# Edge phases of a graph network on one core: no loops, tiles gathered once into a ring, one-hots moved to ScalarE

## The reference

```python
# layer 1, 8 heads
score = einsum('ehd,ehd->eh', q[dst], k[src]) / sqrt(32)
alpha = exp(score - segment_max(score, dst)[dst]) / segment_sum(...)[dst]
out   = segment_sum(alpha[..., None] * v[src], dst)
# layer 3, 4 heads
e   = leaky_relu(e_src[src] + e_dst[dst], 0.2)
a   = exp(e - segment_max(e, dst)[dst]) / segment_sum(...)[dst] * dist
out = segment_sum(ft[src] * a, dst)
```

## Time and profile before

| | |
|---|---|
| median of 3 runs | 9977.47 us |
| the profiled execution | 9991.05 us |
| its span | 9989.3 us |
| busy PE, DVE, POOL, ACT | 73%, 59%, 44%, 34% |
| first edge phase (`att`) | 534 to 3943 us |
| second edge phase (`gat_att`) | 5487 to 8689 us |
| last experts (`sexp`) | 8950 to 9846 us |

### The profile page before, as it was taken

The page is one execution under the profiler, slowest core; times in us unless marked ns, Lnnn a source line. Parts: engine busy times, 40 slices in busy tenths (PEclk is TensorE's granted clock), DMA queues, the critical chain, the costliest instruction groups (busy, mean ns, idle before and its releaser), DMA issues. The chain is left out here.

```text
span 9989.3 us, 143724 instructions
## 1 busy us (share of the span) xinstructions
PE 7296.0 (73%) x33600; PEld 5271.7 (53%) x33600; DVE 5876.5 (59%) x16050; ACT 3420.6 (34%) x10075; POOL 4441.4 (44%) x4446
## 2 busy tenths in 40 slices
PE   3877887887888788535955677777777777659993
PEld 2555555555555555334743444545445545458873
DVE  3467777777777777752124555555555555663332
ACT  1256555555565564222422111111111111222220
POOL 2045555555555553052034655655555556440004
PEclk6989889888898888757977666766676766759996
DMA  4455555555555554444345333333333333335555
GB/s 142 159 151 154 148 153 151 146 151 148 152 153 149 149 151 132 140 144 132 119 143 170 86 81 81 82 81 82 83 82 82 82 82 82 78 118 178 178 178 160
DMA packets 814099, 1276.19 MB, mean 128 GB/s; under 512 B 274566, under 2 KB 585110, under 8 KB 812734
## 3 DMA queue, kind: packets, MB, share of 16 engines
q0 software_dynamic: 272448, 833.22, 30.5%
q1 hardware_dynamic: 540755, 432.95, 14.5%
HBM read 1070.02 MB, written 211.92 MB: 128 GB/s over the span
## 5 line engine op out<-in xcount | busy, mean ns | idle before, releaser
L694 POOL DMA_INDIRECT att_kv<-kv,att_idx x1872 | 1850.1, 988 | 1912.3 <-issue 1475.6
L694 POOL DMA_INDIRECT gat_att_vst<-ft,gat_att_idx x1872 | 1877.6, 1003 | 1340.6 <-DVE gat_att_score L956 723.7
L772 PE MATMUL gat_att_pag<-gat_att_msg,gat_att_S 128*128 128x260 f32 x3744 | 1466.6, 531 | 31.1 <-DVE gat_att_msg L978 9.1
L730 PE MATMUL att_pqd<-sum_acc,att_ST 128*128 x3744 | 1136.1, 431 | 390.9 <-ACT att_ST L816 295.5
L772 PE MATMUL att_pag<-att_msg,att_S 128*128 128x264 f32 x3744 | 1160.5, 436 | 84.4 <-DVE att_msg L978 42.4
L730 PEld LDWEIGHTS att_pqd<-sum_acc,att_ST 128*128 128x128 f32 x3744 | 769.6, 214 | 602.2 <-issue 480.5
L772 PEld LDWEIGHTS gat_att_pag<-gat_att_msg,gat_att_S 128*128 128x128 f32 x3744 | 888.2, 263 | 347.2 <-issue 153.4
L816 ACT CAST gat_att_ST<-gat_att_pST 128x256 bf16<-128x256 f32 x936 | 348.1, 372 | 2110.3 <-remote 1032.9
L772 PEld LDWEIGHTS att_pag<-att_msg,att_S 128*128 128x128 f32 x3744 | 692.6, 206 | 372.6 <-issue 166.9
L727 PE MATMUL gat_att_pqd<-sum_ed,gat_att_ST 128*128 x5616 | 372.1, 171 | 634.0 <-ACT gat_att_ST L816 436.9
L727 PEld LDWEIGHTS gat_att_pqd<-sum_ed,gat_att_ST 128*128 128x128 bf16 x5616 | 335.5, 106 | 941.3 <-issue 860.8
(11 more groups left out here) (474 smaller groups left out, 11913.9 us busy)
## 6 DMA issues: line engine op xcount, KB each, us to landing
sexp_w<-in_L_ffn_w_dram SPq DMA_DIRECT2D x112, 1024.0 KB
att_kv<-kv,att_idx POOLq DMA_INDIRECT x1872
gat_att_vst<-ft,gat_att_idx POOLq DMA_INDIRECT x1872
top_row<-tok SPq DMA_DIRECT2D x106, 256.0 KB
ytok<-top_y SPq DMA_DIRECT2D x106, 256.0 KB
kv<-qkv_row SPq DMA_DIRECT2D x50, 520.0 KB
sexp_row<-stok SPq DMA_DIRECT2D x56, 260.0 KB
sy<-sexp_y SPq DMA_DIRECT2D x56, 256.0 KB
```

Of the source, the lines that this page charges most:

```text
L694: pool.indirect_dma_start(row, None, rows_t, IndirectOffsetOnAxis(ap=idx[:, k, 2 * p + i:2 * p + i + 1], axis=0)).then_inc(s_g[p % R], 16)
L730: t = pe.matmul(pqd[p % 2][:, i * D:i * D + D], lhs, acc[:, bass.ds(b + 1, 1), 0:D], start=True, stop=True)
L772: t = pe.matmul(pag[p % 2][:, 0:AW], S[:, gs % RG, 2 * p + i, :], msg[:, p % 2, i, :], start=(i == 0), stop=(i == 1))
```

## The change

- `prepare_edges` also makes a list of source nodes by tile (`srcN`, one column for each of the 1680 tiles), for each slot pair the place of its tile pair in a ring of 24 and its number, and for each tile pair the number of the last slot pair that uses it (`free`).
- `edge_phase` has no loop any more: all 119 steps of groups are written out on every engine, so that all semaphore values and most addresses are constants.
- In `gat`, POOL gathers each tile pair once (1680 gathers in place of 1872) into a ring of 24 pairs of tiles. It waits for the message of the last slot pair that used the place (`s_msg` against a register from `free`), and tells of arrivals in order, three pairs behind, by a semaphore `s_here`. DVE reads from registers which place holds its slot pair, for the front (`ring`) and for the message (`back`), two slot pairs to a TENSOR_LOAD.
- In `gat`, ACT makes the one-hots as in `att`.
- In `att`, there are two product buffers, and the product waits for the reduction before the last one.
- In `switch_experts` the token rows are issued ahead of the weights.

```diff
+                sp.dma_start(nsrc[0:TN, :, :], dr["src"].rearrange("a (b t e) -> (a t) b e", t=TN, e=P)).then_inc(s_nat, 16)
...
+                    if b < NT // TN:
+                        sp.dma_start(dr["srcN"][:, b * TN:b * TN + TN], tnat[:, s, 0:TN]).then_inc(s_st[s], 16)
+                    if b == 2:
+                        sp.wait_ge(s_ring, 1)
+                        sp.dma_start(dr["ring"].rearrange("(a c) n -> a c n", a=1), ring[:, :, :]).then_inc(s_copy, 16)
+                        sp.dma_start(dr["free"], free[:, :]).then_inc(s_copy, 16)
...
+                    t = pe.transpose(pt[s][:, 2, 0:TBS], natd[0:TBS, s, :], c.ident[0:TBS, 0:TBS])
+                    if b < NT // TN:
+                        t = pe.transpose(pt[s][:, 3, 0:TN], nf[0:TN, s, :], c.ident[0:TN, 0:TN])
+                    t.then_inc(s_turn, 1)
...
+                v.memset(ring[:, :, :], 1).then_inc(s_fill, 1)
...
+                own(v.tensor_tensor(turnf[:, :], fslot[0:1, 0:NS // 2], bfl[:, 1:NS + 1:2], ALU.subtract))
+                own.do(v.tensor_scalar(ring[:, 1, 0:NS // 2], turnf[:, :], 2.0, None, ALU.add))
+                own(v.tensor_scalar(turni[:, 0, :], turnf[:, :], 1.0, None, ALU.add))
+                own(v.tensor_scalar(turni[:, 1, :], turni[:, 0, :], 3, None, ALU.logical_shift_right))
+                own(v.tensor_scalar(turni[:, 2, :], turni[:, 1, :], 171.0, None, ALU.mult))
+                own(v.tensor_scalar(turni[:, 1, :], turni[:, 2, :], 9, None, ALU.logical_shift_right))
+                own(v.scalar_tensor_tensor(ring[:, 0, 0:NS // 2], turni[:, 1, :], -24.0, turni[:, 0, :], ALU.mult, ALU.add))
+                own(v.tensor_scalar(free[:, :], last[:, :], 7, None, ALU.logical_shift_right))
+                own(v.tensor_scalar(free[:, :], free[:, :], float(NBLK - 1), 1.0, ALU.min, ALU.add))
+                own(v.tensor_tensor(free[:, :], free[:, :], islot[0:1, 0:NT // 2], ALU.add))
+                v.sem_inc(s_ring, 1)
+                v.wait_ge(s_nat, 16)
                 for b in range(NIT):
                     s, r = b % 2, slice(0, TBS)
+                    if b < NT // TN:
+                        if b >= 2:
+                            v.wait_ge(s_turn, b - 1)
+                        own(v.tensor_copy(nf[0:TN, s, :], nsrc[0:TN, b, :]))
...
-    UN, HEAD = 18, 8
     LAG = 14
     R = 8 if gat else 4
+    RP, BEHIND = VR * GP, 3
     CD, NCP = 3, 4
+    MC = 128 if gat else 112
...
-        idx = m.sb("idx", [P, RG, G], I32)
+        idx = m.sb("idx", [P, NT] if gat else [P, RG, G], I32)
+        ring = m.sb("ring", [1, RG, 2, GP], I32) if gat else None
+        back = m.sb("back", [1, KR, GP], I32) if gat else None
+        free = m.sb("free", [1, NT // 2], I32) if gat else None
...
-        vst = m.sb("vst", [P, VR, G, VW])
+        vst = m.sb("vst", [P, VR * G, VW])
         kv = None if gat else m.sb("kv", [P, R, 2, RW])
-        prod = None if gat else m.sb("prod", [P, 2 * D])
+        prod = None if gat else m.sb("prod", [P, 2, 2 * D])
...
-            assert (NG - 1 - HEAD) % UN == 0
-            for g in range(HEAD):
-                step(g, g)
-            with eng.Fori(0, (NG - 1 - HEAD) // UN) as it:
-                for j in range(UN):
-                    step(it * UN + (HEAD + j), HEAD + UN + j)
-            for g in range(NG - 1, NG + 2):
+            for g in range(NG + 2):
...
-                    sp.dma_start(idx[:, k, :], dr["srcT"][:, t]).then_inc(s_fl[k], 16)
+                    if gat:
+                        sp.dma_start(ring[:, k, :, :], dr["ring"][:, bass.ds(g * GP, GP)].rearrange(
+                            "(a c) n -> a c n", a=1)).then_inc(s_fl[k], 16)
+                    else:
+                        sp.dma_start(idx[:, k, :], dr["srcT"][:, t]).then_inc(s_fl[k], 16)
...
+                        sp.dma_start(back[:, k, :], dr["ring"][0:1, bass.ds(g * GP, GP)]).then_inc(s_cl[k], 16)
...
+                if gat:
+                    sp.dma_start(idx[:, :], dr["srcN"]).then_inc(s_once, 16)
+                    sp.dma_start(free[:, :], dr["free"]).then_inc(s_once, 16)
...
-                def step(g, gs):
+                def gather_slots(g, gs):
                     if gs >= NG:
                         return
                     k = gs % RG
                     for p in range(GP):
                         T = g * GP + p
                         if p == 0:
-
                             pool.wait_ge(s_fl[k], use(g, gs) * 48)
-                        if gat:
-                            wait(pool, s_front, T - GP + 1)
-                        else:
-                            wait(pool, s_front, T - R + 1)
-                            wait(pool, s_v, T - R + 1)
+                        wait(pool, s_front, T - R + 1)
+                        wait(pool, s_v, T - R + 1)
                         pool.sem_inc(s_go, 1)
                         for i in range(2):
-                            row = vst[:, k, 2 * p + i, :] if gat else kv[:, p % R, i, :]
-                            pool.indirect_dma_start(row, None, rows_t, IndirectOffsetOnAxis(
+                            pool.indirect_dma_start(kv[:, p % R, i, :], None, rows_t, IndirectOffsetOnAxis(
                                 ap=idx[:, k, 2 * p + i:2 * p + i + 1], axis=0)).then_inc(s_g[p % R], 16)
 
-                run(pool, step)
+                def gather_tiles():
+                    pool.wait_ge(s_once, 32)
+                    pool.sem_inc(s_go, 1)
+                    done = None
+                    for t in range(NT // 2 + BEHIND):
+                        if t < NT // 2:
+                            if t >= RP:
+                                f = t - RP
+                                if f % 4 == 0:
+                                    done = nc.values_load_multi_w_load_instructions(
+                                        free[0:1, f:f + 4], engines=[POOL_ENG], min_val=1, max_val=NS)[1]
+                                pool.wait_ge(s_msg, done[f % 4])
+                                pool.sem_inc(s_go, 1)
+                            for i in range(2):
+                                pool.indirect_dma_start(vst[:, t % RP * 2 + i, :], None, rows_t, IndirectOffsetOnAxis(
+                                    ap=idx[:, 2 * t + i:2 * t + i + 1], axis=0)).then_inc(s_g[t % R], 16)
+                        if t >= BEHIND:
+                            pool.wait_ge(s_g[(t - BEHIND) % R], ((t - BEHIND) // R + 1) * 32)
+                            pool.sem_inc(s_here, 1)
+
+                if gat:
+                    gather_tiles()
+                else:
+                    run(pool, gather_slots)
...
-                if not gat:
-                    for p in range(3):
-                        onehot(0, 0, p)
+                for p in range(3):
+                    onehot(0, 0, p)
...
-                        if ahead and not gat:
+                        if ahead:
...
+                place = [None, None]
+
                 def products(g, gs, p):
                     T, b = g * GP + p, gs % 2
-                    v.wait_ge(s_g[p % R], arrived(g, p, R))
+                    if gat:
+                        if p == 0:
+                            v.wait_ge(s_fl[gs % RG], use(g, gs) * 48)
+                            v.sem_inc(s_go, 1)
+                        if p % 2 == 0:
+                            place[0] = nc.values_load_multi_w_load_instructions(
+                                ring[0:1, gs % RG, 0, p:p + 2], engines=[DVE_ENG], min_val=0, max_val=RP - 1,
+                                skip_runtime_bounds_check_because="pair modulo RP by prepare_edges")[1]
+                            place[1] = nc.values_load_multi_w_load_instructions(
+                                ring[0:1, gs % RG, 1, p:p + 2], engines=[DVE_ENG], min_val=1, max_val=NT // 2)[1]
+                        v.wait_ge(s_here, place[1][p % 2])
+                    else:
+                        v.wait_ge(s_g[p % R], arrived(g, p, R))
                     v.wait_ge(s_qd, T + 1)
                     if gat:
                         v.tensor_tensor(score[:, b, :, 2 * p:2 * p + 2].rearrange("p h i -> p i h"),
-                                        vst[:, gs % VR, 2 * p:2 * p + 2, D:D + H],
+                                        vst[:, bass.ds(place[0][p % 2] * 2, 2), D:D + H],
                                         pqd[p % 2][:, 0:2 * H].rearrange("p (i h) -> p i h", i=2),
                                         ALU.add).then_inc(s_front, 1)
                     else:
-                        wait(v, s_score, T)
-                        v.tensor_tensor(prod[:, :].rearrange("p (i d) -> p i d", i=2), kv[:, p % R, :, 0:D],
+                        wait(v, s_score, T - 1)
+                        v.tensor_tensor(prod[:, p % 2, :].rearrange("p (i d) -> p i d", i=2), kv[:, p % R, :, 0:D],
                                         pqd[p % 2][:, :].rearrange("p (i d) -> p i d", i=2),
```

(35 more changed lines are left out.)

53 lines of the change are left out of this document (29 added, 24 removed).

## The result

The changed kernel takes 10,225.9 us (median of 4 runs, 10,217 to 10,238), the kernel before 9,977.2 beside it: ratio 1.025, interval 1.0234 to 1.0266. Slower, outside the range of 9580 to 10,000. Profiled against profiled it is 10,231.4 - 9,991.05 = +240 us.

The account below looks back on a forecast made before the run. DVE bounds quiet stretches of the first edge phase, the order of hand-overs the second. First phase -105 - 60, second +23, experts -50, lists +5: -187 us from 9977.47, so 9790 us; 8-in-10 range 9580 to 10,000.

Parts of the forecast that it names:

- DVE in the second phase: Second edge phase: 458.9 us of one-hots leave DVE, 520 us of register loads come; net 0, bounds -100 to +150.
- -50 us for less traffic: Second edge phase: 192 fewer gathers, POOL off the path, less traffic easing late hand-overs; -50 us, bounds 0 to 100 saved.
- +3: Start of the second phase: POOL waits for the whole list, 4 to 6 us against about 3; +3 us.
- Two product buffers, -105: First edge phase: the wait after the reduction goes, 0.19 us a pair; -105 us, bounds 40 to 178 saved.
- rival C: First edge phase hardly moves, pairs' gains given back at the next hand-over: -30 in place of -165; 9925 us, chance 0.18.
- No loops, -60 and 0: Both edge phases: constants replace register arithmetic; 60 us saved in the first, 0 in the second, bounds 0 to 90 each.
- One-hots on ACT, +70: Second edge phase: one-hots on in-order ACT close a circle that lengthens fast pairs; +70 us, bounds 0 to 280.
- My floor of 2.05 us: Second edge phase: copy, one-hots and PE's transposes form a circle on ACT; no pair faster than 2.05 us.
- Rival A: Second edge phase: ACT's circle decides, 2.4 us a group, plus 1.2 for loads; slower, 10,140 us, chance 0.17.
- Experts, -50: Last experts: rows issued first arrive 5 us earlier, weights about 1.5 later; 50 us saved, 20 if weights lacked slack.
- Preparation, +5: prepare_edges: one more fill, ten more instructions, 14 more stores, copies and transposes; +5 us, bounds 0 to +15.
- My own tests for being wrong: Second phase moves over 150 us either way, or a wait for s_here or on POOL shows ahead of the front.

Follow-up runs that it names:

- e9: Changed kernel with the second phase's gathers by slots again, no ring or loads; ratio 0.9998 where the kernel before takes 9,869 us, second phase 3164 us.
- e11: Kernel before with two product buffers in the first edge phase alone, loops kept; ratio 0.9994 where the kernel before takes 9,869 us.
- e6: Changed kernel, unchanged, run again on a chip where the kernel before takes 9,979 to 10,007 us; ratio 1.0229.
- e8: Changed kernel with fewer, wider register loads, fewer checks and waits, and the experts' old order; ratio 1.0078 where the kernel before takes 9,979 to 10,007 us.
- e12: Changed kernel with wide loads, the experts' old order and DVE making the second phase's one-hots; ratio 1.0041 where the kernel before takes 9,869 us.
- e7: Kernel before without loops in both edge phases and with two product buffers in the first; ratio 0.9884 where the kernel before takes 9,979 to 10,007 us.
- e15: Kernel before without loops and with two product buffers, on a chip where the kernel before takes 8,561 to 8,572 us; ratio 0.9797.
- e5: Kernel before, unchanged, one profiled run on a chip where it takes 9,979 to 10,007 us; edge phases 3384 and 3218 us.
- e4: Changed kernel with fewer, wider register loads, fewer checks and one wait per four pairs; ratio 0.9687 where the kernel before takes 8,561 to 8,572 us.
- e10: Kernel before without loops, with two product buffers and unused register loads with asserts in the second phase; ratio 0.9917 where the kernel before takes 9,869 us.
- e1: Changed kernel with the second phase's gathers by slots again; ratio 0.9769 where the kernel before takes 8,561 to 8,572 us, second phase 2423 us.

## Why the prediction was wrong

**The step that failed** is "DVE in the second phase: relief and loads cancel: 0, bounds -100 to +150". Three things in it were off. The loads' size: I took 13 x 0.342 us a group from the earlier trace rows, the trace has 12 x 0.53 and eight asserts with their arithmetic, 0.213 each: 8.1 us instead of 4.4. Their place: "part is hidden behind the engine's work" compared sums (1310 us of idle time), but the loads stand in line ahead of the very front that PE's next expansion and the chain wait for. In the lines shown the front starts 1.52 us after the addition's end, and two loads with two checks are 1.49 us. And the relief: taking DVE's 458.9 us of one-hots off brought nothing on B (e9 against e11). On A the narrow loads with their checks and waits are 105 us (e6 less e8).

**The rest of the +304 is the ring, and no term of mine priced it.** I gave the gathers -50 us for less traffic. On B a ring with wide loads and DVE's one-hots has 100 us more than the slots (e12, e11); on A the wide ring has 199 more than slots with DVE's one-hots (e8, e7), ScalarE's one-hots among them. Some 24 us of each is the phase's start, 33 in the changed kernel: first to ninth front 72.0 us there, 64.2 in e8 and 62.0 in e12, against 38.6 in the kernel before, 38.0 in e11 and 40 to 43 in e7 and e9; on C it is 18 to 21 for all without spacing. I had +3 for it. Why the ring costs the rest is not shown. What holds TensorE's signals on A and B is not settled either. That it is there is read from two waits of ACT for its turned tile, in e7 on A and e15, the same kernel, on C:

```profile
ACT gat_att_ST L810 <- remote: 1184.8, 307, 16.5
ACT gat_att_ST L810 <- PE gat_att_pST L701: 712.2, 442, 3.5
```
```profile
ACT gat_att_ST L810 <- PE gat_att_pST L701: 1379.0, 815, 5.3
```

"Remote" is gone on C altogether. On A's trace of e5, the late copies (over 1.5 us after the modelled end of their transposes, 314 of them in the second phase) come at the end of a flow of gathered packets: 23.8 in the us before the copy, 12.1 in the us after. That is a correlation; the spacing that would test it never met such a chip. The late hand-overs also account for most of the difference between e4's 541 us on C and 105 on A: what the loads no longer take, they do. Waits of the whole second phase on A, in e6 and then in e8:

```profile
DVE gat_att_score L1030 <- issue: 482.9, 293, 21.1
DVE gat_att_score L1030 <- POOLq L753: 134.0, 88, 3.2
PE gat_att_pqd L788 <- ACT gat_att_ST L877: 367.1, 133, 10.9
DVE sum_acc L1090 <- remote: 58.9, 18, 6.5
```
```profile
DVE gat_att_score L1030 <- issue: 154.1, 143, 13.5
DVE gat_att_score L1030 <- POOLq L753: 1.8, 2, 0.9
PE gat_att_pqd L788 <- ACT gat_att_ST L877: 568.5, 211, 16.5
DVE sum_acc L1090 <- remote: 211.6, 83, 7.6
```

Ahead of the fronts 461 us of waiting go, and 354 us come back where PE waits for the turned tile and DVE for PE's sums. In e7, with slots, PE's wait for that tile is 377.2 us, 191 less than in e8.

**Two product buffers, -105:** mechanism right to the hundredth (0.79 to 0.60, 2.41 to 2.21), size too large: 0 to 20 us on B as a whole kernel (e11), where the loops alone are 53 of the phase; -104 for the phase lies between my -165 and rival C's -30, nearer to mine. That the quiet pairs come earlier to the next late hand-over and wait there, as rival C has it, fits but was not tested.

**No loops, -60 and 0:** 53 us in the first phase, as forecast; 19 (e10 against e11) to 28 us (e7 against e5) in the second, where the rows showed nothing, and where two profiles of one kernel differ by 18. What of it is register arithmetic and what the branch was not separated. The Trainium skill ("Runtime: NRT & Kernel Launch", Instruction fetch mechanics) says that kernels prefer full unrolling where possible, and these two agree with it; no run here shows a stalled fetch.

**One-hots on ACT, +70:** some +30 to +40 on B (e9), and -83 on C (e1 against e15), both with slots; behind the ring it is open. My floor of 2.05 us was wrong: fronts come 1.76 us apart in the changed kernel. The copy that PE needs is of pair T+2, the one-hots behind it are of T+3; the circle spans more than one pair, so that a single pair may be shorter than it. Rival A named the right phase and size of loss (10,140 us) but put most of them on ACT's circle; the loads that it counted beside it (1.2 us a group, 140 us) were nearer to the 105 us measured. That its time is closer than mine is partly luck.

**Experts, -50:** the waits for rows went as forecast, from 103.3 to 47.1 us, and the weights took more than that back: +37. The step that failed is "50 us if they were there in time by that much". From the issue of a tile's transfers to the last update of the semaphores the rows took 10.3 us before and the weights 9.6; changed, the rows take 2.75 and the weights 11.3 (medians of 52 tiles). So the rows were last by 0.7 us only, and the weights land 1.7 us later than they did, where I had 1.5. The queue is not full: it has a packet in flight for 60% of the stage before and 64% after, and stands empty until SP issues the next tile's transfers. The waits for weights are 70.0 us, L2546 itself takes 425.7 us against 404.3 by its group's busy time, and 56.2 us of waits for rows are gone: 70.0 + 21.4 - 56.2 = +35.

**Preparation, +5:** 9, within its bounds.

My own tests for being wrong both struck: the second phase moved by over 150 us, and POOLq L753, which raises `s_here`, stands ahead of fronts with 130.1 us. Of the other signs, ACT is busy for 1592 us (forecast 1730) and a looped group of the first phase takes 28.0 us (27.4).

**The best version** depends on the chip: no loops and two buffers alone beat the kernel before on both chips where they ran, by 1.2 and 2.0% (0.9884 on A, 0.9797 on C). The wide ring with ScalarE's one-hots and the experts' old order is better on C (0.9619 and 0.9646) and loses on A (1.0078).

## What to carry to other kernels

Count a register load where it stands: its time is on the path if the instruction behind it is what another engine waits for, however idle the engine is on the mean. But whether the path is that one has to be measured: 446 us of loads and checks were hidden in e10. Load four values at once and check one, where that is enough; two loads of two took three times as long as one of four. Of transfers that are issued together, one put first is paid for by those behind it, so price both sides of a swap (7.6 us earlier for the rows, 1.7 later for the weights). And a bound made of late hand-overs hides savings and costs alike: ask first whether the other chip shows it.

## What the runs showed of the hardware

- A register load from SBUF on DVE: 0.314 us for one value, 0.528 for two, 0.343 for four; a runtime range check is 0.190 + 0.023 us a value. Two values being the dearest was not expected. The Trainium skill ("DMA: Bandwidth & Descriptors", Latency and other measured facts) gives a floor of about 600 ns; all these rows lie below it, and they decide here.
- The same kernel takes 8,565, 9,869 or 9,990 us by the chip, and the difference is in four stages with many of GpSimd's indirect transfers; two others with such transfers (257 and 134 us) are the same on A and C. On A and B TensorE's results reach ScalarE and VectorE late: for the turned tile 314 of 936 times by over 1.5 us in e5's second phase (median of these 2.7 us, 4.2 in e6), and up to 21 us late in a run of 48 gathers. On C none is (e15, e4). Several of PE's semaphores are then raised at once, mostly as a flow of gather packets ends.
